# A gated recurrent mixer and a Walsh-Hadamard FFN on one core: row parts transposed by the DMA queue instead of TensorE, silu in one activation, new instruction orders

## The chip, the cores and the metric

The program runs on one core of a Trainium2 chip. The metric is the device time of one execution in microseconds. The core has TensorE (PE in the profile; its weight loads are PEld), VectorE (DVE), ScalarE (ACT), GpSimd (POOL) and SyncE (SP), which here issues every DMA.

## The reference

Input x is 4 batches x 512 rows x 512 columns, float32. With LN the layer norm without gain:

```
h = LN(x)
i, f, g = h Wi^T, h Wf^T, h Wg^T                 # 512 -> 512 each
gate = sigmoid(f);  v = silu(i) * (1 - gate)
o[t] = gate[t] * o[t-1] + v[t]                   # scan over the 512 rows of a batch
o = o * rsqrt(mean(o^2) + eps) * gnorm * g * sigmoid(g)
x = x + LN(o Wo^T)
z = LN(x)
hidden = fwht(silu(z W1^T) * (z W3^T))           # 512 -> 2048, Walsh-Hadamard over 2048
x = x + LN(hidden W2^T)                          # 2048 -> 512
```

## The kernel before, in words

**Numbers.** A float32 operand of a product is split into two float16 parts, high and low (low = value - high), and a product is three float16 passes into one PSUM bank: high x high, high x low, low x high (three_passes, L576 to L579). The transform fwht is folded into W2 once, in eight units (FW on GpSimd, H2 on TensorE, ScalarE and VectorE).

**Order.** Each engine runs a list of steps that stands written out at the top (PE_ORDER, ACT_ORDER, DVE_ORDER, POOL_ORDER, SP_ORDER, L37 to L186). A step is KIND.batch.index; in PE_ORDER a number behind a colon is its PSUM bank. Every step waits on semaphores for what it needs, and what stands behind it in its list waits with it. SP's list too is run in order, its waits included.

**Steps of a batch on TensorE.** XT transposes four 128-row tiles of normalised rows against the identity, in float32, four 128x128 blocks a tile. F, I and G (4 each) are the projections, 12 matmuls of 512 columns; MS sums squares; Y (4) is the product with Wo. ZT transposes the rows of the second norm. In batch 0, GA and UP (16 each, 12 matmuls) are the products with W1 and W3. In batches 1 to 3 each pair of column chunks is computed by seven products of half size, Strassen-Winograd's way: GP (6 matmuls of 256 columns), GQ, GR and GU (12 each), for 16 steps g, and ZT has seven steps: three of the rows' quarters and four of sums that GpSimd makes (ZA). D (64 a batch, three matmuls of 512 columns) is the product with W2.

**Around them.** Behind an XT or ZT step ScalarE copies the bank as the high part and VectorE subtracts for the low part, into xb or ring (L844, L932, L935; L1065, L1188, L1191). ScalarE computes sigmoid of F, I, G and GA (L869, L879, L901, L991); VectorE multiplies I, G and GA by their sigmoid (L1128, L1145, L1302), scans (S, L1140), multiplies the gate in (P, L1152). UP: VectorE multiplies, ScalarE rounds, GpSimd takes the low part (L1417). Row norms: VectorE's bn_stats (X1, Y, Z1, V), a GpSimd power (L1345), then VectorE or ScalarE applies them.

**Weights of the later batches.** SL loads the float32 weights of a chunk pair into comb_raw (L530), GpSimd forms four sums in place (SA, L1407 to L1413), ScalarE and VectorE split them (SH, SO), SS stores them to w_comb in DRAM; AS stores the plain parts. WL loads 1792 KB a pair into one of three slots of ring (L548).

**Other waits that matter.** The hidden parts of chunks 2 to 5 of batch 0 lie in xb[1], so batch 1's rows may be written there only after the sixth chunk's D (L842). GA.0.0 needs all of ZT.0, the weight scales (WS on VectorE) and WT.0.0. H2.0.0 needs neg_had (HN, L1288). GpSimd's unit 3 reuses the buffer of unit 0 and waits for H2.0.1 (L1386).

Of the kernel before, what the change touches and what calls it, by code (L numbers as in the profile page):

```python
# [42 lines left out]
GA.0.3:5 D.0.0 D.0.1 D.0.2 D.0.3 D.0.4 D.0.5 D.0.6 D.0.7 UP.0.3:6 D.0.8 D.0.9 D.0.10 D.0.11 GA.0.4:7 UP.0.4:5
D.0.12 D.0.13 D.0.14 D.0.15 GA.0.5:4 D.0.16 D.0.17 D.0.18 D.0.19 UP.0.5:6 GA.0.6:7 UP.0.6:5 GA.0.7:4 D.0.20
D.0.21 D.0.22 D.0.23 XT.1.0:6 XT.1.1:7 XT.1.2:5 XT.1.3:4 D.0.24 D.0.25 D.0.26 D.0.27 F.1.0:6 I.1.0:7 G.1.0:5
I.1.1:4 F.1.1:6 G.1.1:7 I.1.2:5 F.1.2:6 G.1.2:4 I.1.3:7 F.1.3:5 G.1.3:6 UP.0.7:4 GA.0.8:7 UP.0.8:5 D.0.28 D.0.29
D.0.30 D.0.31 MS.1.0:6 Y.1.0:4 Y.1.1:7 D.0.32 D.0.33 D.0.34 D.0.35 Y.1.2:5 Y.1.3:6 GA.0.9:4 UP.0.9:7 GA.0.10:5
UP.0.10:6 GA.0.11:4 D.0.36 D.0.37 D.0.38 D.0.39 ZT.1.0:7 ZT.1.1:5 ZT.1.2:6 UP.0.11:4 D.0.40 D.0.41 D.0.42 D.0.43
ZT.1.3:7 ZT.1.4:4 ZT.1.5:5 GA.0.12:6 D.0.44 D.0.45 D.0.46 D.0.47 ZT.1.6:7 UP.0.12:4 GA.0.13:5 UP.0.13:6 D.0.48
D.0.49 D.0.50 D.0.51 GA.0.14:7 UP.0.14:4 GA.0.15:5 UP.0.15:7 XT.2.0:6 XT.2.1:4 XT.2.2:5 D.0.52 XT.2.3:7 D.0.53  # L50
D.0.54 D.0.55 D.0.56 F.2.0:6 I.2.0:4 G.2.0:5 I.2.1:7 F.2.1:6 G.2.1:4 I.2.2:5 F.2.2:7 G.2.2:6 D.0.57 D.0.58
D.0.59 D.0.60 I.2.3:4 F.2.3:5 D.0.61 G.2.3:7 D.0.62 D.0.63 GP.1.0:6 GQ.1.0:4 GR.1.0:5 GP.1.1:6 GQ.1.1:7 GU.1.0:6
MS.2.0:4 Y.2.0:7 GR.1.1:5 GP.1.2:4 GQ.1.2:6 GP.1.3:4 GU.1.1:5 GQ.1.3:6 GR.1.2:7 Y.2.1:4 GR.1.3:5 GU.1.2:7
GP.1.4:6 D.1.0 GQ.1.4:5 GU.1.3:6 GP.1.5:7 Y.2.2:4 GQ.1.5:7 GR.1.4:6 GP.1.6:5 D.1.1 D.1.2 GQ.1.6:6 GR.1.5:5
GU.1.4:7 GP.1.7:4 D.1.3 Y.2.3:5 GQ.1.7:7 GR.1.6:4 D.1.4 GU.1.5:6 D.1.5 GP.1.8:5 GQ.1.8:4 GR.1.7:6 GU.1.6:5
GP.1.9:7 D.1.6 GQ.1.9:6 GR.1.8:7 GU.1.7:5 D.1.7 D.1.8 D.1.9 GR.1.9:5 D.1.10 D.1.11 D.1.12 D.1.13 D.1.14 D.1.15
D.1.16 D.1.17 D.1.18 GU.1.8:4 D.1.19 D.1.20 D.1.21 GP.1.10:7 GQ.1.10:6 GU.1.9:4 GP.1.11:5 GQ.1.11:7 GR.1.10:5
GP.1.12:4 GQ.1.12:6 GR.1.11:4 GU.1.10:5 GP.1.13:7 GQ.1.13:4 GR.1.12:5 GU.1.11:7 D.1.22 D.1.23 D.1.24 GP.1.14:7
D.1.25 D.1.26 D.1.27 D.1.28 D.1.29 D.1.30 D.1.31 D.1.32 D.1.33 D.1.34 GQ.1.14:6 GR.1.13:7 D.1.35 GU.1.12:5
# [24 lines left out]
D.3.55 D.3.59 D.3.63
# [103 lines left out]
def mixer_ffn_kernel(nc, x, w_i, w_f, w_g, w_o, gnorm, w_13t, w_2t, eye, hadamard, out):  # L188
# [15 lines left out]
    with ExitStack() as ctx:  # L204
# [370 lines left out]
        def _(pe):  # L575
# [885 lines left out]
```

## Time and profile before

| | us |
|---|---|
| median of 3 runs (731.03 to 731.64) | 731.22 |
| the profiled execution, whole | 729.96 |
| its span in the trace | 728.2 |
| PE busy / PEld busy | 700.3 (96%) / 427.9 |
| DVE busy | 519.2 (71%) |
| ACT busy | 285.4 (39%) |
| POOL busy | 311.1 (43%) |

Busy times are sums of instruction durations in the span. Matmuls overlap: one begins before the one ahead has ended, so a PE busy share near 100% says that it never ran dry, and the distance of starts says what a matmul costs. The chain of waits follows the last instruction back to what released it, step by step.

### The profile page before, as it was taken

What the parts mean: (1) busy time and instruction counts of PE and PEld (TensorE: products, weight loads), DVE (VectorE), ACT (ScalarE), POOL (GpSimd) and SP (SyncE); (2) the same over time, 40 slices, a digit from 0 to 9 for tenths busy, and PEclk for the clock granted to TensorE, in tenths of its full rate; (3) what the DMA queues carried; (4) which work ended last, traced back from release to release, by engine and by line L of the source; (5) the groups of instructions that cost most, each with busy time, mean ns of one, the idle gap of its engine ahead of it and who ended that gap; (6) DMA issues with size and microseconds to landing.
All of it is one profiled execution on the core that took longest, in us unless ns stands there. A gap on an engine that the chain in (4) does not pass through costs nothing.

```text
span 728.2 us, 11322 instructions
## 1 busy us (share of the span) xinstructions
PE 700.3 (96%) x4280; PEld 427.9 (59%) x4280; DVE 519.2 (71%) x877; ACT 285.4 (39%) x482; POOL 311.1 (43%) x268
## 2 busy tenths in 40 slices
PE   4898789999999999999999999999999999999996
PEld 2443334445444545467778677556666768876762
DVE  6997799895756765688755576885657765756564
ACT  5677844564443334343221332442312233313221
POOL 2967799453667843324341212241224530203112
PEclk9999979999999999999999999999999999999999
DMA  8961243364326475054252272432223332472002
GB/s 333 417 240 58 79 133 108 121 240 159 116 116 228 163 229 205 1 174 136 111 217 102 102 260 103 138 137 86 84 101 112 146 141 68 165 261 102 30 1 87
DMA packets 28199, 105.73 MB, mean 145 GB/s; under 512 B 2800, under 2 KB 7152, under 8 KB 23536
## 3 DMA queue, kind: packets, MB, share of 16 engines
q1 hardware_dynamic: 28144, 105.00, 40.7%
q8 instruction: 34, 0.56, 0.3%
q14 instruction: 21, 0.17, 0.1%
HBM read 81.92 MB, written 23.07 MB: 144 GB/s over the span
## 4 chain that ended last, share of the span: by engine, by line
PE 92%; DVE 4%; issue 1%; DMA 1%; ACT 0%; DVEq 0%; POOL 0%; SPq 0%
PE ps L577 28%; PE ps L578 28%; PE ps L579 28%; PE ps L751 2%; PE ps L752 2%; DVE ring L1086 1%; PE ps L719 1%; PE ps L629 1%; DVE st L1047 1%; DMA rows<-L_attn_hidden_states 1%; PE ps L686 0%; DMA x1r<-x_rows 0%; DVEq L1048 0%; DVE rows L1182 0%; DVE exps L1071 0%
## 5 line engine op out<-in xcount | busy, mean ns | idle before, releaser
L577 PE MATMUL ps<-xb,ring 128*128 128x256 f16 (+1 forms) x704 | 225.9, 321 | 0.1
L579 PE MATMUL ps<-xb,ring 128*128 128x256 f16 (+1 forms) x704 | 225.9, 321 | 0.0
L578 PE MATMUL ps<-xb,ring 128*128 128x256 f16 (+1 forms) x704 | 225.9, 321 | 0.0
L577 PEld LDWEIGHTS ps<-xb,ring 128*128 128x128 f16 x704 | 69.0, 98 | 45.9 <-issue 1.6
L578 PEld LDWEIGHTS ps<-xb,ring 128*128 128x128 f16 x704 | 68.9, 98 | 45.4 <-issue 1.0
L579 PEld LDWEIGHTS ps<-xb,ring 128*128 128x128 f16 x704 | 68.9, 98 | 42.1
L1345 POOL TENSOR_TENSOR rstd<-var,neg_half 128x1 f32<-128x1 f32 x64 | 43.8, 687 | 115.3 <-DVE var L1323 50.7
L1417 POOL TENSOR_TENSOR hsp<-sga,hsp 128x512 f16<-128x512 f32 x34 | 41.6, 1230 | 115.6 <-ACT hsp L1005 115.4
L579 PE MATMUL ps<-ring 128*128 128x256 f16 x288 | 78.5, 273 | 0.0
L577 PE MATMUL ps<-ring 128*128 128x256 f16 x288 | 78.5, 273 | 0.0
L578 PE MATMUL ps<-ring 128*128 128x256 f16 x288 | 78.5, 273 | 0.0
L1255 DVE TENSOR_TENSOR ring<-ps,ring 128x512 f32<-128x512 f32 x48 | 33.1, 689 | 29.7 <-PE ps L579 29.6
L991 ACT ACTIVATE sga<-ring,gate_c 128x512 f32<-128x512 f32 x48 | 34.5, 720 | 47.7 <-DVE ring L1266 36.1
L969 ACT ACTIVATE junk<-ps 128x256 f32<-128x256 f32 x48 | 18.4, 384 | 86.2 <-PE ps L579 86.2
L1302 DVE SCALAR_TENSOR_TENSOR sga<-ring,gate_c,sga 128x512 f32<-128x512 f32 x48 | 38.4, 803 | 19.0 <-ACT sga L991 19.0
L577 PE MATMUL ps<-w2t,hsp 128*128 128x512 f16 x136 | 51.5, 379 | 0.0
L578 PE MATMUL ps<-w2t,hsp 128*128 128x512 f16 x136 | 51.5, 379 | 0.0
L579 PE MATMUL ps<-w2t,hsp 128*128 128x512 f16 x136 | 51.5, 379 | 0.0
L1266 DVE TENSOR_TENSOR ring<-ps,ring 128x512 f32<-128x512 f32 x48 | 33.1, 689 | 25.8 <-PE ps L579 24.9
L1417 POOL TENSOR_TENSOR ring<-sga,ring 128x512 f16<-128x512 f32 x22 | 25.6, 1181 | 55.0 <-ACT ring L1005 55.0
L1245 DVE TENSOR_TENSOR ring<-ps,junk 128x512 f32<-128x512 f32 x48 | 32.9, 688 | 16.4 <-PE ps L579 13.7
L1314 DVE SCALAR_TENSOR_TENSOR sga<-ring,up_c,sga 128x512 f32<-128x512 f32 x48 | 41.2, 862 | 1.4 <-issue 0.2
(190 smaller groups left out, 1326.4 us busy)
## 6 DMA issues: line engine op xcount, KB each, us to landing
ring<-w_comb SPq DMA_DIRECT2D x24, 1792.0 KB, 7.3
ring<-W13t SPq DMA_DIRECT2D x16, 512.0 KB, 10.4
ring<-W13t SPq DMA_DIRECT2D x8, 1024.0 KB, 6.4
w_comb<-ring SPq DMA_DIRECT2D x8, 1024.0 KB, 8.5
rows<-L_attn_hidden_states SPq DMA_DIRECT2D x16, 256.0 KB, 4.0
w2t<-W2t SPq DMA_DIRECT2D x8, 512.0 KB, 13.6
res<-L_attn_hidden_states SPq DMA_DIRECT2D x16, 256.0 KB, 4.0
x_rows<-res SPq DMA_DIRECT2D x16, 256.0 KB, 3.0
```

The costliest lines, as they stand in the source:

```text
L577: pe.matmul(dst, a_hi, b_hi, start=start, stop=False)
L578: pe.matmul(dst, a_hi, b_lo, start=False, stop=False)
L579: return pe.matmul(dst, a_lo, b_hi, start=False, stop=stop)
L969: act.activation(p_copy[:, g % 2], bank("GP", b, g)[:, 256:512], ACT.Copy).then_inc(sp_rdy, 1)
L991: act.activation(sga[:, c % 2], src, ACT.Sigmoid, scale=gate_c[:]).then_inc(sga_rdy, 1)
L1245: dve.tensor_tensor(combined(g % 2)[:, 0:512].rearrange("p (o t) -> p o t", o=2), bank("GQ", b, g)[:].rearrange("p (o t) -> p o t", o=2), ...
L1255: dve.tensor_tensor(to[:, 512:1024].rearrange("p (o t) -> p o t", o=2), bank("GR", b, g)[:].rearrange("p (o t) -> p o t", o=2), both, ALU. ...
L1266: dve.tensor_tensor(to[:, 512:1024], bank("GU", b, g)[:], to[:, 512:1024], ALU.add).then_inc(gu_rdy, 1)
L1302: dve.scalar_tensor_tensor(sga[:, c % 2], src, gate_c[:], sga[:, c % 2], ALU.mult, ALU.mult).then_inc(sil_rdy, 1)
L1314: dve.scalar_tensor_tensor(sga[:, c % 2], src, up_c[:], sga[:, c % 2], ALU.mult, ALU.mult).then_inc(hid_rdy, 1)
L1345: pool.tensor_tensor(dst, src, neg_half[:].broadcast_to(src.shape), ALU.pow).then_inc(done, 1)
L1417: pool.tensor_tensor(hid(b, c, 1), sga[:, c % 2], hid(b, c, 0), ALU.subtract).then_inc(hid_lo, 1)
```

## The change

Batch 0 keeps its transposes on TensorE. In batches 1 to 3:

- XT and ZT on ScalarE and VectorE now split rows that are not transposed yet, in SBUF, into scratch of the attention part (si, sg, o_s, osq, osum, gate). SP then issues transposing DMAs, XD (4 a batch, 128 x 1024 float16 each) and ZD (7 a batch, each two of 128 x 512), into xb and ring. TensorE's 12 XT and 21 ZT steps of these batches are gone; F waits for XD, GP for ZD, and ScalarE's XT of batches 2 and 3 for all ZD of the batch before.
- GA, I and G use Silu, and VectorE's multiply by the sigmoid is gone; their bank is free after ScalarE. P multiplies the gain in as well. F's gate is 0.5 * tanh(f / 2) + 0.5 in two ScalarE steps.
- comb_raw has two places, ring slots 32 and 56 in turn. The three slots of WL are permuted.
- A few one-column VectorE steps change from three operands to two.
- All five orders are new.

```diff
+            def transpose_x(b, t):
+                sp.wait_ge(xt_lo, TC * b + t + 1)
+                if b == 1 and t == 0:
+                    sp.wait_ge(d_mm, EARLY)
+                if b > 1 and t == 0:
+                    sp.wait_ge(up_mm, HC * (b - 1))
+                sp.dma_start_transpose(xb[:, b % 2].rearrange("p s k t -> p (s k) t")[:, :, chunk(t)],
+                                       parts_of_x(t).rearrange("p s d -> p (s d)")).then_inc(ld_xt, 16)
+            def transpose_z(b, q):
+                sp.wait_ge(z_lo, z_count(b, q))
...
+                for i in range(2):
+                    sp.dma_start_transpose(place_of_z(b, q, i), parts_of_z(q)[:, i].rearrange("p s d -> p (s d)")
+                                           ).then_inc(ld_zt, 16)
 # TensorE
             def f(b, c):
+                if c == 0 and b > 0:
+                    pe.wait_ge(ld_xt, 16 * TC * b)
             def products_p1(b, g):
-                    pe.wait_ge(z_hi, z_count(b, 6))
-                    pe.wait_ge(z_lo, z_count(b, 6))
+                    pe.wait_ge(ld_zt, 32 * 7 * b)
 # ScalarE
             def xt(b, t):
+                if b > 0:
+                    act.wait_ge(x_norm, TC * b + t + 1)
+                    if b > 1:
+                        act.wait_ge(ld_zt, 32 * 7 * (b - 1))
+                    act.activation(parts_of_x(t)[:, 0], rows[:, t], ACT.Copy).then_inc(xt_hi, 1)
+                    return
             def f(b, c):
-                act.activation(gate[:, c % 2], bank("F", b, c)[:], ACT.Sigmoid, scale=unscale[:, 0:1]
+                act.activation(gate[:, c % 2], bank("F", b, c)[:], ACT.Tanh, scale=unscale[:, 0:1]
+                               ).then_inc(tanh_rdy, 1)
+                act.wait_ge(tanh_rdy, n + 1)
+                act.activation(gate[:, c % 2], gate[:, c % 2], ACT.Identity, bias=half[:], scale=0.5
                                ).then_inc(gate_rdy, 1)
-                act.activation(sga[:, c % 2], src, ACT.Sigmoid, scale=gate_c[:]
+                act.activation(sga[:, c % 2], src, ACT.Silu, scale=gate_c[:]
 # VectorE
             def xt(b, t):
+                if b > 0:
+                    dve.tensor_tensor(parts_of_x(t)[:, 1], rows[:, t], parts_of_x(t)[:, 0], ALU.subtract
+                                      ).then_inc(xt_lo, 1)
+                    return
-            def ga(b, c):
-                n = HC * b + c
-                dve.wait_ge(sga_rdy, n + 1)
-                src = combined(0)[:, c % 2 * 512:c % 2 * 512 + 512] if b > 0 else bank("GA", b, c)[:]
-                dve.scalar_tensor_tensor(sga[:, c % 2], src, gate_c[:], sga[:, c % 2],
-                                         ALU.mult, ALU.mult).then_inc(sil_rdy, 1)
 # weight sums, SP
                 if j == 0:
                     sp.wait_ge(up_mm, 2)
                     sp.wait_ge(st_a[0], 32)
+                elif j == 1:
+                    sp.wait_ge(up_mm, 8)
+                    for i in range(2):
+                        sp.wait_ge(st_a[i], 64)
                 else:
-                    sp.wait_ge(s_lo, 2 * j)
+                    sp.wait_ge(s_lo, 2 * j - 2)
```

From the new orders, the places that the prediction names:

```
PE_ORDER   XT.0.0:4 AN.0.0:5 XT.0.1:6 ... F.0.0:5 W2N.3.0 I.0.0:4 GC.0.0:6 F.0.1:1 ...
           G.0.1:5 AN.3.0:6 H2.0.0:4 H2.0.1:1 H2.1.0:7 I.0.2:2 F.0.2:3 F.0.3:6 G.0.2:0 I.0.3:5 H2.1.1:2
           G.0.3:4 H2.2.0:3 H2.2.1:6 H2.3.0:0 MS.0.0:5 Y.0.0:4 Y.0.1:1 Y.0.2:7 Y.0.3:2 ZT.0.0:5 H2.3.1:3
           H2.4.0:4 WS.0.0:1 H2.4.1:6 ZT.0.1:7 ZT.0.2:2 ZT.0.3:5 H2.5.0:1 H2.5.1:7 GA.0.0:2 UP.0.0:5 ...
           D.0.23 GA.0.8:4 D.0.24 ... D.0.28 UP.0.8:5 GA.0.9:6 F.1.0:7 I.1.0:4 ... MS.1.0:5 Y.1.0:6 Y.1.1:4
           Y.1.2:5 Y.1.3:7 D.0.36 D.0.37 UP.0.11:6 D.0.38 ... D.0.43 GA.0.12:4 UP.0.12:5 GA.0.13:6 D.0.44 ...
           GA.0.14:4 D.0.52 UP.0.14:5 GA.0.15:6 UP.0.15:7 D.0.53 ... D.0.61 GP.1.0:4 GQ.1.0:5 ... F.2.0:4
ACT_ORDER  AQ.0.0 XT.0.0 AQ.1.0 AT.0.0 XT.0.1 AQ.2.0 XT.0.2 XT.0.3 ... UP.0.15 XT.2.0 XT.2.1 XT.2.2 GP.1.0
DVE_ORDER  ... AT.0.2 HN.0.0 W2S.0.0 ... Z2.0.2 ZT.0.0 Z2.0.3 WS.0.0 ZT.0.1 ZT.0.2 ZT.0.3 WT.0.0 ...
POOL_ORDER ... P.0.0 FW.3.0 FW.3.1 FW.3.2 FW.3.3 FW.3.4 S.0.1 P.0.1 FW.3.5 ... Z1.0.3 FW.5.3 FW.5.4 FW.5.5 ...
SP_ORDER   ... SL.1.0 SL.2.0 AS.5.0 XD.1.0 XD.1.1 XD.1.2 XD.1.3 SL.3.0 ... ZD.1.0 ... ZD.1.5 XL.2.0 XL.2.1
           ZD.1.6 XL.2.2 XL.2.3 WL.1.0 WL.1.1 WL.1.2 XD.2.0 XD.2.1 XD.2.2 XD.2.3 WL.1.3 ...
```

## Rows read from the trace of the kernel before

**Rows 1.** The chain that ended last, by engine: share of the span.

```profile
PE 92%; DVE 4%; issue 1%; DMA 1%; ACT 0%; DVEq 0%; POOL 0%; SPq 0%
```

**Rows 2.** Stretches: length, busy time and instructions by engine, granted clock, DMA share, GB/s.

```profile
core 0: us, PE busy (x) PEld busy (x) DVE busy (x) ACT busy (x) POOL busy (x), PEclk, DMA share, GB/s
20.00:60.00 40.00, 35.07 (x190) 17.12 (x189) 38.95 (x58) 28.23 (x58) 29.82 (x20) 0.99 0.79 306
80.00:100.00 20.00, 13.31 (x44) 6.89 (x42) 18.29 (x51) 11.11 (x23) 17.16 (x18) 0.75 0.52 159
100.00:720.00 620.00, 620.00 (x3920) 388.09 (x3920) 432.29 (x701) 216.32 (x348) 239.55 (x206) 1.00 0.38 132
```

**Rows 3.** Timeline of PE, D steps near the end: start, duration, line, tile.

```profile
717.14 0.38 PE L579 MATMUL ps<-w2t,xb 128*128 128x512 f16 x1
...
719.08 0.38 PE L579 MATMUL ps<-w2t,xb 128*128 128x512 f16 x1
```

**Rows 4.** The chain in order of time: start, time on the chain, what.

```profile
594.48 0.44 PE ps L719 x4
...
639.98 0.11 PE ps L577
```

**Rows 5.** Groups by line and shape: busy us, mean ns, idle before; TensorE's transposes.

```profile
L629 PE MATMUL ps<-ident,rows 128*128 128x128 f32 x80 | 13.8, 319 | 15.2 <-DVE rows L1060 8.5 <-DVE rows L1182 6.7
L719 PE MATMUL ps<-ident,res 128*128 128x128 f32 x48 | 6.5, 273 | 0.0
L719 PE MATMUL ps<-ident,rows 128*128 128x128 f32 x36 | 5.1, 272 | 0.0
```

**Rows 6.** Groups by line and shape: the other engines' steps.

```profile
L1302 DVE SCALAR_TENSOR_TENSOR sga<-ring,gate_c,sga 128x512 f32<-128x512 f32 x48 | 38.4, 803 | 19.0 <-ACT sga L991 19.0
L1152 DVE TENSOR_TENSOR sg<-sg,o_s 128x512 f32<-128x512 f32 x16 | 16.2, 1014 | 0.2
L1128 DVE SCALAR_TENSOR_TENSOR si<-ps,unscale,si 128x512 f32<-128x512 f32 x16 | 11.9, 747 | 14.9 <-ACT si L879 14.9
L1407 POOL TENSOR_TENSOR ring<-ring 128x512 f32<-128x512 f32 x8 | 10.9, 1357 | 6.5 <-DMA ring<-W13t 6.5
L913 ACT ACTIVATE ot<-sg 128x512 f16<-128x512 f32 x16 | 10.0, 622 | 2.9 <-DVE sg L1152 2.7
```

**Rows 7.** DMA issues: count, KB each, median us from issue to landing.

```profile
ring<-w_comb SPq DMA_DIRECT2D x24, 1792.0 KB, 7.3
ring<-W13t SPq DMA_DIRECT2D x16, 512.0 KB, 10.4
rows<-L_attn_hidden_states SPq DMA_DIRECT2D x16, 256.0 KB, 4.0
ring<-L_attn_Wf SPq DMA_DIRECT2D x1, 1024.0 KB, 6.6
```

**Rows 8.** Line L514 (SP's weight loads): issue duration ns min/median/max, first and last start.

```profile
L514 SPq DMA_DIRECT2D ring<-W13t x16: 327/433/2936, 17.8 to 55.3; - x16
```

**Rows 9.** Timeline of PE before and at GA.0.0, with idle time before and its releaser.

```profile
58.71 1.55 PE L751 MATMUL ps<-x1r,had 128*128 128x512 f32 x2 [3.31 <-issue]
...
82.44 1.02 PE L751 MATMUL ps<-x1r,had 128*128 128x512 f32 x2
83.30 1.02 PE L752 MATMUL ps<-x1r,had 128*128 128x512 f32 x2
...
95.03 1.09 PE L629 MATMUL ps<-ident,rows 128*128 128x128 f32 x4 [0.83 <-DVE rows L1182]
...
101.71 0.38 PE L577 MATMUL ps<-xb,ring 128*128 128x512 f16 x1
```

**Rows 10.** Timeline of DVE: neg_had, and the first weight's low part.

```profile
58.40 0.22 DVE L1288 TENSOR_SCALAR neg_had<-had 128x128 f32<-128x128 f32 x1
...
100.49 1.08 DVE L1224 SCALAR_TENSOR_TENSOR ring<-ring,w_s 128x512 f16<-128x512 f32 x1
```

**Rows 11.** Timeline of POOL: the first step of unit 3.

```profile
64.23 2.51 POOL L1392 TENSOR_TENSOR x1r<-w2t 128x512 f32<-128x512 f32 x2 [2.16 <-PE ps L752]
```

**Rows 12.** Groups by line and shape: ScalarE's table loads.

```profile
L836 ACT ACT_TABLE_LOAD x1 | 1.3, 1283 | 0.7 <-PEq L1436 0.7
```

More of the change, by code:

```diff
@@ L43 @@
[L43 to L47, printed above, removed]
@@ L216, in mixer_ffn_kernel @@
         neg_half = sb("neg_half", [P, 1])
+        half = sb("half", [P, 1])
         warm = sb("warm", [P, 1])
@@ L343, in comb_z, with parts_of_x, parts_of_z, rows_of_z @@
             return flat[:, at:at + 512].rearrange("p (k t) -> p k t", k=2)
+        def parts_of_x(t):
+            return (si, sg, o_s, osq)[t][:].bitcast(F16).rearrange("p (s d) -> p s d", s=2)
+        def parts_of_z(q):
+            flat = (gate[:, 0], gate[:, 1], si[:], sg[:], o_s[:], osq[:], osum[:])[q]
+            return flat.bitcast(F16).rearrange("p (i s d) -> p i s d", i=2, s=2)
+        def rows_of_z(q):
+            if q > 2:
+                return comb_rows(q)
+            tiles, half = (0, 0, 2)[q], (0, 1, 1)[q]
+            return rows[:, tiles:tiles + 2, 256 * half:256 * half + 256]
+        def place_of_z(b, q, i):
+            if q < 4:
+                flat, at = xb[:, b % 2].rearrange("p s k t -> p (s k t)"), 1024 * q
+            else:
+                flat, at = ring, (98 if b % 2 else 40) * KB + 1024 * (q - 4)
+            return flat[:, at:at + 1024].rearrange("p (m t) -> p m t", m=4)[:, :, chunk(i)]
         def z_count(b, q):
@@ L704, in zt @@
                 wait_bank("ZT", b, t)
-                if b == 0:
-                    pe.wait_ge(z_norm, t + 1)
-                    transpose_tile(bank("ZT", b, t), rows[:, t]).then_inc(z_mm, 1)
-                    return
-                dst = bank("ZT", b, t)
-                if t < 3:
-                    pe.wait_ge(z_norm, TC * b + (4 if t == 2 else 2))
-                    tiles, half = (0, 0, 2)[t], (0, 1, 1)[t]
-                    src = rows[:, tiles:tiles + 2, 256 * half:256 * half + 256]
-                else:
-                    pe.wait_ge(z_cmb, TC * (b - 1) + t - 2)
-                    src = comb_rows(t)
-                for k in range(2):
-                    for i in range(2):
-                        last = pe.transpose(dst[:, 256 * k + P * i:256 * k + P * (i + 1)], src[:, i, chunk(k)], ident[:])
-                last.then_inc(z_mm, 1)
+                pe.wait_ge(z_norm, t + 1)
+                transpose_tile(bank("ZT", b, t), rows[:, t]).then_inc(z_mm, 1)
             def ws(b, t):
@@ L834, in _ @@
         def _(act):
-            act.wait_ge(half_set, 1)
-            act.activation(warm[:], neg_half[:], ACT.Sigmoid)
+            act.wait_ge(half_set, 2)
+            act.activation(warm[:], neg_half[:], ACT.Silu)
             def xt(b, t):
-                act.wait_ge(xt_mm, TC * b + t + 1)
-                if b == 1 and t == 0:
-                    act.wait_ge(d_mm, EARLY)
-                if b >= 2 and t == 0:
-                    act.wait_ge(up_mm, HC * (b - 1))
+                if b > 0:
[4 more added lines that the diff above has]
+                    return
+                act.wait_ge(xt_mm, t + 1)
                 act.activation(xb[:, b % 2, 0, :, chunk(t)], quarters(bank("XT", b, t)), ACT.Copy).then_inc(xt_hi, 1)
@@ L878, in i @@
                     act.wait_ge(o_rdy, n)
-                act.activation(si[:], bank("I", b, c)[:], ACT.Sigmoid, scale=unscale[:, 1:2]
+                act.activation(si[:], bank("I", b, c)[:], ACT.Silu, scale=unscale[:, 1:2]
                                ).then_inc(sgi_rdy, 1)
@@ L900, in g @@
                     act.wait_ge(o_lo, n)
-                act.activation(sg[:], bank("G", b, c)[:], ACT.Sigmoid, scale=unscale[:, 2:3]
+                act.activation(sg[:], bank("G", b, c)[:], ACT.Silu, scale=unscale[:, 2:3]
                                ).then_inc(sgg_rdy, 1)
```

417 lines of the change are left out of this document (209 added, 208 removed).

## The prediction, made before the changed kernel was run

> **What bounds the kernel now.** I read the shares of the chain first, then the stretches, then TensorE's own gaps. The chain that ended last is 92% TensorE [rows 1]. The stretches say where the rest lies: from 100 to 720 us TensorE is busy for all 620.00 us at the full clock, while VectorE is busy for 432 and ScalarE for 216 of them [rows 2]. In that part only less TensorE work makes the kernel shorter; a faster VectorE, ScalarE or GpSimd gives nothing there. Before 100 us it is different: PE is busy 13.31 of 20 us between 80 and 100, at a granted clock of 0.75, and VectorE 38.95 of 40 between 20 and 60 [rows 2].
>
> What TensorE's work costs is read from starts, not durations: a 512-column matmul lasts 0.38 us, but ten starts lie 1.94 apart, 0.2155 each [rows 3]; a 256-column one takes 0.11 of the chain [rows 4]. So F, I, G, Y, GA and UP are 12 x 0.2155 = 2.59 us each, D 0.65, GP 0.66, GQ, GR and GU 1.31 each; H2, two times 0.86 between starts [rows 9], 1.72. Four transposes take 0.44 us of the chain [rows 4]. Adding these along PE_ORDER, GA.0.0 stands at 72 us and the end at 692; in the trace GA.0.0 starts at 101.7 and the last work ends near 721.6. So 29.5 us are lost before GA.0.0 and next to nothing behind it.
>
> **Transposes off TensorE.** Removed: 3 batches x 4 XT steps x 4 = 48 and 3 x 7 ZT steps x 4 = 84 transposes, together 132; the 84 are the two forms of L719, and 48 of the 80 of L629 [rows 5]. 132 x 0.109 = 14.4 us. All of it stands where TensorE never idles, so all of it counts, if nothing is late in its place.
>
> The split moves ahead of the transpose: ScalarE copies rows instead of a bank (0.62 us, L913's form), and VectorE subtracts with both operands in SBUF; its nearest row is L1152, 1.01 us instead of 0.69 [rows 6]. 33 x 0.33 = +11 us of VectorE, against far more taken away below.
>
> **What the transposes cost the queue.** XD is 256 KB, ZD two transfers of 128 KB. The trace has no transposing transfer. Call c the queue's time for 256 KB. From below: 306 GB/s were moved on the mean of 20 to 60 us [rows 2], so 0.86 us; a queue that does nothing else may be somewhat quicker. From above: 512 KB of W13t take 10.4 us to landing, so 5.2 us for 256 KB [rows 7]. I take 1.3 us, nearer the lower end: a single 256 KB tile lands in 4.0 us [rows 7], most of it latency that four issued together share. What c may be is read from the work that stands between in the new orders:
> - XD.1 may start when D.0.23 is done (it writes where the early hidden chunks lie). Up to F.1.0 stand GA.0.8, UP.0.8, GA.0.9 and five D: 51 matmuls, 11.0 us, for 4c. At 1.3 plus a landing of 3 that is 8 us: hidden, and the tightest place.
> - Y.1.3 to GP.1.0: nine GA/UP and 26 D, 40.1 us. The norm chain takes some 14 us to the first split rows (in batch 0 the last ZT can start at 95.03 [rows 9], 12.6 us after the last Y's end at 82.44; GpSimd's row sums come behind that, while the first parts are already on their way). Then 7c, and behind them on the same queue WL.1.0, a w_comb load of 7.3 us [rows 7]. 14 + 7c + 7.3 = 30 us: hidden.
> - XD.2: UP.0.15 to F.2.0 is 37.6 us, with three w_comb loads ahead (22 us): leaves 15 for 4c. XD.3: GU.1.15 to F.3.0 26.7 us, two loads ahead: leaves 12. ZD.2 and ZD.3: 56 and 67 us.
>
> SP gets 54 more issues. By its plain issue, 0.43 us [rows 8], they are 23 us over 728; an upper end is the 2.9 us of its slowest one [rows 8], 157 us, still a fifth of the span. The new waits hold what is behind them: WL.1.0 waits behind ZD.1.6, and ScalarE's XT.2.0 waits for all ZD.1 with GP.1.0's copy behind it. GP.1.0 needs both anyway.
>
> The Trainium skill is at odds with itself here. "VectorE: DVE Perf Modes" (The three transpose paths) gives 390 ns for a 128x128 block on TensorE and 1309 ns through the DMA; eight blocks would make c 10.5 us. "Advanced Engine Details and Errata" (X-Bar Transpose) calls them as fast as regular DMAs. The trace prices TensorE's block at 109 ns, not 390, so I trust the first page's figures little as rates; no run here shows either yet.
>
> **One-activation gates.** GA loses its multiply (48 x 0.803 and 16 from a bank at L1128's 0.747, 50.5 us), I and G theirs (L1128's 11.9, and as much for G) [rows 6]: VectorE sheds 74 us and gains 11. F gets a second ScalarE pass, 16 x 0.62 = 10 us (L913's copy is the nearest) [rows 6]. Behind 100 us TensorE hides both signs: worth 0. If that cover were gone, the 0.62 would sit on the way to each scan.
>
> **Raw pairs.** The second buffer (over ring slots 56 to 63, free after UP.0.7) lets a load overlap four GpSimd sums of 1.36 or a little more each; GpSimd waited only 6.5 us in all for eight loads [rows 6]. Nothing of it is on the chain: worth 0, bounds -1 to +1 us. What it needs is that SS.7 is done before WL.1, 40 us earlier in TensorE's work than before (GP.1.0 moves from 286 to 247 in the sum). From UP.0.7 to there stand 121 us of work; seven pairs at about 6 us each take 42. Enough.
>
> **New orders, before GA.0.0.** Up to F.0.0 I expect nothing: Wf is issued behind four x tiles and lands 6.6 us later [rows 7], so squaring it first starts it little earlier, and XT.0.0 now stands behind it; bounds -1 to +1 us. Two gaps do change:
> - 3.31 us up to 58.71 [rows 9]. H2.0.0 waited for neg_had, written at 58.40 behind VectorE's gate work [rows 10]. In the new DVE_ORDER HN stands early and four H2 halves stand before G.0.3. The gap goes, and with it the slow clock behind it (two passes take 1.55 us there [rows 9]; about 1 us in all). What is late next is the gate chain: G.0.3 to ScalarE 0.7, VectorE 1.0, copy 0.6, GpSimd 1.4 and hand-overs, about 5; three H2 and MS (5.95 us) cover it. Gain 4.5 us.
> - From the last Y's end (82.44) to GA.0.0 at 101.71 [rows 9] are 19.3 us with 8.8 of work. VectorE's weight scales, two low parts and WT.0.0, done at 101.57 [rows 10], stand last. The new order leaves them there, so the time stays about 17.5, but 10.5 us of work stand in it (one more H2). GpSimd's unit 5 must be done by then: in the trace its unit 3 started only at 64.23, waiting for H2.0.1 [rows 11]; this now comes earlier. Idle falls from 10.5 to about 7: gain 3 us.
> Together 7 us, at the ends 2 (only the first gap, paid partly elsewhere) and 10.
>
> **Sum.** The profiled execution is 729.96 us, its span 728.2. 729.96 - 14.4 - 7 = 708.6, plus 1 us for a first wait at F.1.0 that the window of 11 us may just let through: 709.6. The median of the runs is 731.22, 1.26 above the profiled execution, so 710.9: **711 us**. Own range 704 to 718.
>
> **Rivals.**
> 1. *The queue's transposes are slow and TensorE waits for them.* For it: no row prices a transposing transfer, four in 11 us is tight, and loads queue behind them. Against: DMA is only 0.38 busy from 100 to 720 [rows 2]. Waits: F.1.0 4c - 11, GP.1.0 7c - 18.7, F.2.0 4c - 15, F.3.0 4c - 12. At the upper end, c = 5.2, that is 9.8 + 17.7 + 5.8 + 8.8 = 42: 711 + 42 = 753. It cancels the gain of 20 from c = 4.1 (5.4 + 10 + 1.4 + 4.4 = 21), so from about 4.2 us for 256 KB the kernel is slower. By the Trainium skill's 1309 ns a block (the page above) the same sum, with ZD.2 and ZD.3 late too, would give about 920; I give that 0.03 of the chance below. A mild form (c about 3.3) costs 8 to 10 us: 720.
> 2. *Silu and Tanh are not in one ScalarE table.* Then each F and the I behind it reload: 32 loads of 1.283 us [rows 12]. In batch 0 eight of them, 10.3 us, fall where ScalarE is busy 28.23 of 40 us [rows 2]; later ones are covered. About 8 us: 719. Against: in the trace one load serves Sigmoid, Square, Copy and Identity for the whole run [rows 12], so a table holds several functions. The Trainium skill's "ScalarE: Activation LUTs" (Table sets) names tanh beside sigmoid and does not place silu.
> 3. *The orders before GA.0.0 give nothing* (F.0.0 later since XT waits behind AQ.0.0, GpSimd's sixth unit late for H2.5): only the 14.4 stay: 717 to 718.
>
> **Chances.** Forecast 0.58, orders give nothing 0.12, mild queue wait 0.06, table 0.05, slow queue (above the old time) 0.19. Under 0.2% nothing can be told from no change (1.5 us); only a sliver between the mild and the slow queue lies there, 0.03, taken half from the slow case. So faster 0.79, same 0.03, slower 0.18. The range reaches from 703 into the slow case, to 738.
>
> **What would show it.** In the trace after: no L629/L719-like transposes after batch 0; TensorE busy in full from GA.0.0 to the end; its end near 700. GA.0.0 at about 95 to 98 us instead of 101.7 (its place in the new order is 3.4 us later, so the loss falls from 29.5 to 22). No gap before the first H2; Y.0.0 near 69. Landing of XD under 5 us and no TensorE wait on it at F.1.0; one table load. Wrong if TensorE idles at F.1.0 or GP.1.0 for the transposes, if more table loads appear, or if GA.0.0 is not earlier.

## The result, and the profile after

The changed kernel takes 721.78 us (median of 4 runs, 718.46 to 722.41) beside 731.12 us for the kernel before on the same chip: a ratio of 0.9867, 95% interval 0.9833 to 0.9901. It is faster by 9.3 us, where 20.2 were forecast. A second series on another chip gave 721.84 us, ratio 0.9888 (0.9872 to 0.9903). The profiled execution is one of 722.41 us, so the traces differ by 7.5 us.

The page of the changed kernel, busy time and share of the span by engine, then the chain that ended last by engine:

```profile
PE 689.6 (96%) x4148; PEld 414.3 (57%) x4148; DVE 469.3 (65%) x782; ACT 290.4 (40%) x498; POOL 322.2 (45%) x268
...
PE 77%; POOL 9%; DVE 5%; DMA 3%; issue 2%; SPq 2%; ACT 1%; POOLq 0%; DVEq 0%; ACTq 0%
```

TensorE held 92% of the chain [rows 1]; now it is 77%, and GpSimd has 9% where it had none. The same three stretches as in [rows 2]:

```profile
core 0: us, PE busy (x) PEld busy (x) DVE busy (x) ACT busy (x) POOL busy (x), PEclk, DMA share, GB/s
20.00:60.00 40.00, 34.27 (x171) 16.86 (x169) 36.46 (x53) 26.24 (x51) 33.02 (x22) 0.91 0.73 286
80.00:100.00 20.00, 16.21 (x60) 7.98 (x58) 16.88 (x49) 13.54 (x35) 17.96 (x19) 0.83 0.19 66
100.00:720.00 620.00, 610.44 (x3797) 374.17 (x3795) 390.28 (x634) 224.49 (x370) 246.51 (x206) 0.99 0.47 152
```

From 100 us on TensorE is no longer full. The stretch from 80 to 100 is fuller (16.21 us for 13.31), the one from 20 to 60 is not (34.27 for 35.07), and there the clock has fallen to 0.91.

To find each gap, the start of every step of PE_ORDER was laid against the price that the prediction gives it; what lies between two starts beyond that price is idle TensorE or slow clock. From the first instruction to the end of the last matmul:

| | before | after |
|---|---|---|
| GA.0.0 starts at | 101.7 | 105.2 (its place is 3.4 of work later) |
| lost before it | 29.5 | 29.6 |
| from GA.0.0 to the end | 620.0 | 609.3 |
| lost in that part | 0 | 7.3 |
| end | 721.7 | 714.5 |

Behind GA.0.0: 620.0 - 3.4 (H2.5, now ahead of it) - 14.4 + 7.3 = 609.5. The transposes' 14.4 us are there in full. The new orders won nothing before GA.0.0, and 7.3 us are newly lost behind it, in waits and in the slow clock after them: 6.0 from MS.1.0 to Y.1.2 at 226 to 236 us, 1.3 at D.0.56 at 281 us.

One trace tells the first part only roughly. The nine traces of kernels that have the changed kernel's early steps (it was profiled twice, and seven of the experiments below leave these steps alone) start GA.0.0 between 102.2 and 105.9 us, at 104.2 on the mean, and F.0.0 between 19.0 and 21.5. So the new early orders may be worth about 1 us, not 7.

The chain of waits of the changed kernel through the first of the new waits, in order of time (start, time on the chain, what):

```profile
175.73 1.16 ACT ring L1004
176.91 1.07 DVE ring L1266
178.11 1.29 DVE ring L1266
179.42 8.99 DMA ring<-W13t
188.47 2.13 POOL ring L1436
...
216.72 2.13 POOL ring L1440
218.93 1.60 POOL ring L1442
220.53 2.04 POOL ot L1392
222.56 1.11 POOL hsp L1446
223.68 1.69 POOL osum L1387
225.45 0.64 ACT osq L940
226.15 1.41 POOL osum L1387
227.70 1.02 PE ps L744 x8
228.73 1.03 issue
229.75 0.59 PE ps L633
230.34 0.43 PE ps L634
```

L1436 to L1442 are GpSimd's four passes of a weight sum (SA). The chain runs along them from 161.8 to 222: a sum, its split, the load of the next raw pair, the next sum. L1392 and L1387, the gate's low part (P) and the sum of squares (S) for which MS.1.0 and Y.1.0 wait, stand in the same queue behind SA.5 and SA.6. Two matmuls of TensorE in a row then start 0.43 us apart, twice the 0.2155 of [rows 3]: after the wait the clock is down. Stretches of the same trace around both large waits:

```profile
core 0: us, PE busy (x) PEld busy (x) DVE busy (x) ACT busy (x) POOL busy (x), PEclk, DMA share, GB/s
...
38.00:42.00 4.00, 0.00 (x0) 0.00 (x0) 3.93 (x5) 0.52 (x1) 3.92 (x3) 0.90 0.63 250
42.30:47.30 5.00, 5.00 (x14) 1.97 (x15) 3.16 (x7) 4.41 (x11) 2.83 (x3) 0.50 0.00 0
...
230.00:234.80 4.80, 4.80 (x12) 1.67 (x11) 0.00 (x0) 0.00 (x0) 4.56 (x4) 0.50 0.89 331
```

At a granted clock of 0.50, the 1.2 GHz level, a wait of 4.4 us at 38 to 42 costs 2.5 more behind it, and the two that make 3.0 before 230 (1.7 at MS.1.0, 1.3 at Y.1.0) cost 3.0.

### The profile page after: what moved, and what is told of

Read it like the earlier page. It is cut to its first block, busy times and chain, and to the rows that moved or that the text cites. A ratio compares the mean times of both kernels' runs of the same rounds, so it can differ in the third digit from the quotient of the medians.

```text
span 720.6 us, 11006 instructions
## 1 busy us (share of the span) xinstructions
PE 689.6 (96%) x4148; PEld 414.3 (57%) x4148; DVE 469.3 (65%) x782; ACT 290.4 (40%) x498; POOL 322.2 (45%) x268
## 4 chain that ended last, share of the span: by engine, by line
PE 77%; POOL 9%; DVE 5%; DMA 3%; issue 2%; SPq 2%; ACT 1%; POOLq 0%; DVEq 0%; ACTq 0%
PE ps L633 24%; PE ps L634 24%; PE ps L635 24%; PE ps L795 1%; PE ps L796 1%; DVE ring L1135 1%; SPq L563 1%; POOL ring L1440 1%; POOL ring L1438 1%; POOL ring L1436 1%; DMA ring<-W13t 1%; POOL ring L1442 1%; DMA ring<-L_attn_Wf 1%; POOL rstd L1374 1%; POOL ot L1392 1%
## 5 line engine op out<-in xcount | busy, mean ns | idle before, releaser
L1374 POOL TENSOR_TENSOR rstd<-var,neg_half 128x1 f32<-128x1 f32 x64 | 40.3, 638 | 103.8 <-DVE var L1100 38.6
L1446 POOL TENSOR_TENSOR hsp<-sga,hsp 128x512 f16<-128x512 f32 x34 | 42.0, 1238 | 98.5 <-ACT hsp L1049 98.5
L1446 POOL TENSOR_TENSOR ring<-sga,ring 128x512 f16<-128x512 f32 x22 | 26.1, 1193 | 100.4 <-ACT ring L1049 100.4
L1092 DVE BATCH_NORM_STATS2 st<-ps 128x6 f32<-128x512 f32 x32 | 22.2, 695 | 30.0 <-PE ps L635 30.0
L1392 POOL TENSOR_TENSOR ot<-sg,ot 128x512 f16<-128x512 f32 x16 | 24.2, 1515 | 34.2 <-ACT ot L961 34.1
```

Of the source, the lines that this page charges most:

```text
L1092: dve.bn_stats(st[:, which], src)
L1374: pool.tensor_tensor(dst, src, neg_half[:].broadcast_to(src.shape), ALU.pow).then_inc(done, 1)
L1392: pool.tensor_tensor(ot[:, 1, c, :], sg[:], ot[:, 0, c, :], ALU.subtract).then_inc(o_lo, 1)
L1446: pool.tensor_tensor(hid(b, c, 1), sga[:, c % 2], hid(b, c, 0), ALU.subtract).then_inc(hid_lo, 1)
```

## The experiments

Ratios are to the kernel before on the same chip; in us against its median there (729.6 to 730.2).

**Three transposes of four left out of the kernel before.**

```diff
-                for k in range(KC):
+                for k in range(first, KC):      # first = KC - 1 in batches 1 to 3; the ZT steps alike
```

> The kernel before, with one TensorE transpose instead of four in each of the 33 transposing steps of batches 1 to 3 (the splits read the one transposed quarter four times; three quarters of the transposed values are left out). Theory: TensorE has no idle time from GA.0.0 on, so each transpose is worth its 0.109 us and 99 of them 10.8 us: 720.3 us against 731.1. Rival (the slots of the transposes are covered by waits for the split, so the change got its 9.3 us elsewhere): within 2 us of 731.1.

Measured: 721.53 us, 0.9885 (0.9872 to 0.9898), 8.1 less. In its trace a step that was 0.44 us apart from the next is 0.11 in 26 of 33 cases, and the end comes 8.9 us earlier. So 0.109 is the price. The 1.9 us that came back stand right behind the other seven steps; for 0.8 of them the trace names what was waited for, a hidden part or a split, as here ahead of D.0.24 (timeline of PE: start, duration, line, idle before and its releaser):

```profile
166.16 0.60 PE L632 MATMUL ps<-ident,rows 128*128 128x128 f32 x4
167.27 0.38 PE L580 MATMUL ps<-w2t,hsp 128*128 128x512 f16 x1 [0.50 <-POOL hsp L1420]
```

**The gates alone, in the kernel before.** Sigmoid becomes Silu (I, G, GA) or Tanh and Identity (F), and DVE_ORDER loses its I, G and GA; Tanh's argument isn't halved.

> The kernel before, with the gates alone changed: Tanh and Identity for F, Silu for I, G and GA on ScalarE, VectorE's products I, G and GA left out (GS folded as in the changed kernel). Theory (VectorE is off the path that sets the end once TensorE is saturated; before GA.0.0 it is not): after GA.0.0 nothing; before it, VectorE's chain is 8 products x 0.7 to 1.7 us shorter and Y and Z start earlier: 727 to 731 us (before 730 to 731). Rival (gates are where the gain comes from): 722 to 725.

Measured: 729.19 us, 0.9987 (0.9978 to 0.9995): 0.4 to 1.6 us less, all of it before GA.0.0 (100.5 us for 101.7, though F.0.0 came 2.9 us later in that trace; why is open). VectorE's 74 us are worth nothing behind it.

**The old orders before GA.0.0, in the changed kernel.** The first splice put H2.5.0 directly ahead of GA.0.0, the second behind UP.0.0:

```diff
-... ZT.0.3:5 H2.5.0:1 H2.5.1:7 GA.0.0:2 UP.0.0:5 GA.0.1:0 ...
+... ZT.0.3:0 H2.4.0:1 H2.4.1:3 GA.0.0:7 UP.0.0:4 H2.5.0:2 H2.5.1:6 GA.0.1:0 ...
```

> The changed kernel, with the orders of the kernel before up to GA.0.0 on TensorE, ScalarE and VectorE and up to FW.4.5 on GpSimd (VectorE's gate products left out, as in the changed kernel). Theory (the new orders before GA.0.0 are worth nothing): idle TensorE before GA.0.0 as in the changed kernel, 29 to 30 us, GA.0.0 at 101 to 102 with H2.5.0 and H2.5.1 behind it: 721 to 722 us. Rival (the new early orders do give the 7 us that the prediction took): 727 to 729.

> The changed kernel with the orders of the kernel before up to GA.0.1 on TensorE and ScalarE, up to WT.2.0 on VectorE (gate products and X1.1.x left out) and up to FW.4.5 on GpSimd. In the first such run H2.5.0 stood directly ahead of GA.0.0 and waited 4.9 us there, which neither kernel has; here it stands behind UP.0.0, as in the kernel before. Theory (new early orders worth nothing): idle TensorE before GA.0.1 as in the changed kernel, 30 us: 721 to 722 us. Rival (worth some us): 724 to 728.

Measured: 724.85 us (0.9930), with 4.9 us of waits at H2.5.0 and H2.5.1 that neither kernel has; and 722.22 us, 0.9891 (0.9878 to 0.9904), beside 0.9888 of the changed kernel. GA.0.0 starts at 101.1 us and H2.5's 3.4 come behind it: 104.5 against 105.2. The new early orders are worth nothing, shown from that side.

**The early order mended.** On VectorE, W2D.0.0 waited behind a split (AT.1.2) and a scan (S.0.0):

```diff
-... GS.0.0 AT.1.2 S.0.0 W2D.0.0 AT.0.2 HN.0.0 ...
+... GS.0.0 W2D.0.0 AT.1.2 S.0.0 AT.0.2 HN.0.0 ...      # first run; and X2.0.0 before X1.0.3
+... AT.2.0 HN.0.0 ... GS.0.0 W2D.0.0 AT.1.2 S.0.0 ...  # second; X1/X2 as they were; PE: H2.3.1 before ZT.0.0
```

> The changed kernel, with two steps of VectorE's written order moved: X2.0.0 before X1.0.3 (as in the kernel before), and W2D.0.0 before AT.1.2 and S.0.0. Theory: the new early order pays back what it wins, at XT.0.0 (10.2 us against 8.2) and at W2S.0.0 (4.4 us of idle TensorE, then about 2.5 us at half clock). XT.0.0 is back at 8.2, the wait at W2S.0.0 goes; part of it comes back as a wait at H2.0.0 or the Z phase: 717.8 us, 4 less than the changed kernel (2 to 9 less). Rival (the stretch before GA.0.0 is bound by the chain of VectorE, ScalarE and GpSimd, whatever TensorE does): within 1 us of 721.8, GA.0.0 at 105.

> The changed kernel, with W2D.0.0 before AT.1.2 and HN.0.0 behind AT.2.0 on VectorE, and H2.3.1 before ZT.0.0 on TensorE. The run with W2D.0.0 moved and X2.0.0 back showed the wait at W2S.0.0 gone, a new one of 3.8 us at H2.0.0 for HN.0.0, and the wait at XT.0.0 only handed to AN.0.0. Theory: without HN's wait GA.0.0 starts at 97 (105.2 in the changed kernel, 102.1 in that run): 714 us. Rival (the chain of scans and splits on VectorE sets MS.0.0, and TensorE waits there instead): GA.0.0 at 101 to 103, 718 to 720.

Measured: 719.78 us, 0.9858 (0.9838 to 0.9878), and 720.51 us, 0.9874 (0.9860 to 0.9888). In the first trace the 4.4 + 2.5 us at W2S.0.0 are gone and H2.0.0 waits 3.8 + 1.6 for neg_had; GA.0.0 at 102.1. In the second neither waits, TensorE is busy for 39.62 of 40 us from 20 to 60, and MS.0.0 waits 3.6, then 3.4 at half clock; GA.0.0 at 104.5. The three traces with the first edit (that of the first run and two of the kernels that join the moves, below) start GA.0.0 at 101.4 to 102.6 us, 2.2 earlier on the mean than the nine without it. The second run's time is that of its rival. The wait moves along VectorE's chain: MS.0.0 waits for the fourth scan (66.06 to 68.13 us) and its square and sum, and VectorE is busy 38.91 of the 40 us:

```profile
20.00:60.00 40.00, 39.62 (x209) 19.69 (x207) 38.91 (x53) 28.02 (x54) 36.77 (x24) 1.00 0.71 276
```

**The last weight sums behind the Y phase of batch 1.**

```diff
-... UP.0.8 P.1.0 SA.5.0 P.1.1 S.1.1 SA.6.0 P.1.2 UP.0.9 S.1.2 S.1.3 S.2.0 P.1.3 SA.7.0 Y.1.0 ...
+... UP.0.8 P.1.0 P.1.1 S.1.1 P.1.2 UP.0.9 S.1.2 S.1.3 S.2.0 P.1.3 SA.5.0 Y.1.0 ... ZA.1.6 SA.6.0 UP.0.12 SA.7.0 UP.0.13
+... the same to ZA.1.6, then UP.0.12 SA.6.0 UP.0.13 SA.7.0           # second run
+... and UP.0.14 before X1.2.1, UP.0.15 before X1.2.3                 # third run
```

> The changed kernel, with the weight sums SA.5, SA.6 and SA.7 (and their SH, SO, SL, SS steps) behind P.1.3 and the Y phase of batch 1 in every engine's order, otherwise the same. Theory: MS.1.0 and Y.1.x wait for GpSimd's P.1.x and S.1.x, queued behind the sums; with them gone the 6 us between MS.1.0 and Y.1.2 go (1.7, 1.3, and 2.5 + 0.5 at half clock): 715.8 us. Rival (the sums then end too late: GQ.1.0 waits for the last store, at 284 us): 721 to 726, with a gap at GQ.1.0. Second rival (P.1.x is bound by ScalarE and VectorE, not by GpSimd's queue): 721.8, MS.1.0 still at 227.

> The changed kernel, with the weight sums SA.5 behind P.1.3, SA.6 behind UP.0.12 and SA.7 behind UP.0.13 on GpSimd, and their SH and SO steps behind the ZT and UP steps of their engines, so that neither the P, S, Y steps of batch 1 nor UP.0.12 stand behind a sum. Theory: in the first try with late sums the 6 us at MS.1.0 and Y.1.x did go, and came back as 13 us at D.0.48 and D.0.52, since SH.6.0 stood ahead of UP.0.12 and ZT.1.4 on ScalarE; without that only the first effect is left: 716 us, 5 to 6 less than the changed kernel. Rival (the sums and the transposing DMAs need all of the time up to GP.1.0, so every order has a wait of some 6 us somewhere before it): 720 to 724, with a gap between D.0.48 and GQ.1.0.

> As the run with the last weight sums set apart, and besides: on GpSimd UP.0.14 before X1.2.1 and UP.0.15 before X1.2.3, on ScalarE SH.7.0 behind UP.0.14, on VectorE SO.7.0 behind X1.2.3. In that run the stall at MS.1.0 and Y.1.x was gone and D.0.56 waited 4.2 us, and 2.4 us at half clock, for UP.0.14 on GpSimd, which stood behind the x statistics of batch 2. Theory (both waits are matters of the written order, and the work fits before GP.1.0): 714.5 to 716 us. Rival (the next one is GQ.1.0 or GP.1.2, for the last stored sum and the load behind it, since the chain of sums has no more room): 719 to 722.

Measured: 727.16 us (0.9961), 720.80 us (0.9880, 0.9862 to 0.9898), 719.59 us (0.9853, 0.9838 to 0.9868). In all three the 6 us from MS.1.0 to Y.1.2 are gone. The first lost 14.6 us from D.0.48 to GA.0.15, since ScalarE's SH.6.0 stood ahead of ZT.1.4 and UP.0.12. The second lost 6.6 at D.0.56. Its GpSimd (timeline: start, duration, line, idle before) did the x statistics of batch 2, L1371, ahead of UP.0.14, the L1443 at 273.94:

```profile
272.38 0.55 POOL L1371 TENSOR_TENSOR rstd<-var,neg_half 128x1 f32<-128x1 f32 x1 [4.32 <-DVE var L1097]
273.42 0.55 POOL L1371 TENSOR_TENSOR rstd<-var,neg_half 128x1 f32<-128x1 f32 x1 [0.50 <-DVE var L1097]
273.94 1.15 POOL L1443 TENSOR_TENSOR hsp<-sga,hsp 128x512 f16<-128x512 f32 x1
```

The third still waits 0.6 us at D.0.52 and 2.4 at D.0.60, and the 1.7 lost from D.0.61 to GR.1.0 are slow clock behind that wait:

```profile
280.40:283.50 3.10, 3.10 (x15) 2.00 (x14) 2.45 (x9) 0.38 (x1) 0.00 (x0) 0.50 1.03 431
```

So more than half of the 6 us came back before GP.1.0 was through, and the time is that of the rival; its cause is not seen there. VectorE waited 2.5 us for the store of the last sums, TensorE not at all.

**GpSimd's sums cut to 8 of 128 columns.**

> The changed kernel, with GpSimd's four passes of each weight sum on 8 of 128 columns per quarter (the sums are left out, all instructions and waits stay). Theory (GpSimd's 52 us of sums hold MS.1.0, and run beside VectorE they slow both engines: its pass took 1.26 us alone and 2.13 beside VectorE's, VectorE's split 1.24 to 2.2): the 7.3 us of idle TensorE after GA.0.0 go down to the 1.3 of D.0.56 or less, SO's pass on VectorE falls from 2.2 towards 1.3: 715.5 us. Rival (MS.1.0 waits for the scans of VectorE and ScalarE, not GpSimd): 720 to 722.

Measured: 716.15 us, 0.9804 (0.9791 to 0.9818), some 6 us below the changed kernel's 0.9888. The waits from MS.1.0 to Y.1.2 are gone and 3.0 us are left at D.0.56 and GP.1.0. Between the two profiled executions lie 4.5 us. The split behind the sums gets shorter on VectorE though it is untouched, by lines and shapes the changed kernel's and then this one's:

```profile
L1266 DVE SCALAR_TENSOR_TENSOR ring<-ring,w_s 128x1024 f16<-128x1024 f32 x16 | 30.6, 1950 | 2.3 <-ACT ring L1004 2.3
```

```profile
L1266 DVE SCALAR_TENSOR_TENSOR ring<-ring,w_s 128x1024 f16<-128x1024 f32 x16 | 23.4, 1505 | 6.1 <-ACT ring L1004 6.1
```

**One raw pair at a time.** One wait changed, and the same wait added for the second pair, which give a load the pace of a single buffer; SL.2.0 stands behind XD.1.3:

```diff
-                    sp.wait_ge(s_lo, 2 * j - 2)
+                    sp.wait_ge(s_lo, 2 * j)
```

> The changed kernel, where each load of a raw pair waits until the pair before it is summed and split (as with a single buffer), SL.2.0 put behind XD.1.3. Theory (the prediction's: the second pair is worth nothing in itself): within 1 us of the changed kernel. Rival (the sums' chain ends at the Y phase of batch 1, so each load of 4.5 to 9 us that is no longer hidden makes it later): 4 to 15 us slower, with the gap at GQ.1.0 or MS.1.0.

Measured: 754.13 us, 1.0331 (1.0317 to 1.0345): 32 us slower than the changed kernel beside it, twice the upper end of what the rival expected. The chain alternates between load and sum (start, time on the chain, what):

```profile
188.99 6.42 DMA ring<-W13t
195.48 1.27 POOL ring L1437
196.82 1.27 POOL ring L1439
198.16 1.27 POOL ring L1441
199.51 1.27 POOL ring L1443
200.81 1.16 ACT ring L1005
201.99 2.49 DVE ring L1267 x2
204.49 6.29 DMA ring<-W13t
```

15.5 us a pair; ScalarE waits for each sum with G and F queued behind. In these orders the second pair is necessary. With orders written for one pair it might cost less; that wasn't tried.

**The transposing DMAs in halves.**

```diff
-                sp.dma_start_transpose(xb[:, b % 2].rearrange("p s k t -> p (s k) t")[:, :, chunk(t)],
-                                       parts_of_x(t).rearrange("p s d -> p (s d)")).then_inc(ld_xt, 16)
+                for s in range(2):      # the ZD steps alike
+                    sp.dma_start_transpose(xb[:, b % 2, s, :, chunk(t)], parts_of_x(t)[:, s]).then_inc(ld_xt, 16)
```

> The changed kernel with each transposing DMA cut in two (the high and the low parts apart): the same bytes and blocks, 108 transfers instead of 54. Theory (about 1.3 us of the queue for each transfer, whatever its size): in batch 1 the ZD steps take 28 x 1.27 = 36 us of the queue instead of 18, and what stands behind them, the x loads with UP.0.14 and GP.1.0, is 18 us late, of which 1 to 3 us were waited already: 736 to 742 us, with the waits at D.0.56 or GP.1.0; F.1.0 5 us late besides, since four XD have 11 us and now take 10.6 and a landing. Rival (time by bytes): 720 to 723.

Measured: 760.00 us, 1.0408 (1.0385 to 1.0431). D.0.56 waits 19.7 us, F.1.0 2.1, and 15.3 more, which the theory did not give, stand in batch 2 from D.1.40 to D.1.46. The queue of SP (start, time, line, count), the changed kernel's XD and the halves' ZD of batch 1:

```profile
169.31 1.34 SPq L548 DMA_TRANSPOSE xb<-si  x1
171.09 1.23 SPq L548 DMA_TRANSPOSE xb<-sg  x1
```

```profile
256.25 11.58 SPq L564 DMA_TRANSPOSE xb<-gate  x8
267.88 5.11 SPq L564 DMA_TRANSPOSE xb<-si  x4
```

256 KB take 1.24 us on the median, 128 KB 1.27 (and in the chain below), 64 KB 1.25: the queue is charged for the transfer, not for its bytes.

**What stands behind the transposes on the queue.** The chain of the changed kernel before D.0.56:

```profile
272.05 1.19 SPq L563
273.28 1.27 SPq L563
274.60 2.96 DMA rows<-L_attn_hidden_states
277.59 0.69 DVE st L1092
278.80 0.55 POOL rstd L1374
279.35 1.13 POOL hsp L1446
```

The last ZD issues (L563), then an x tile of batch 2, its statistics on VectorE and GpSimd, and only then UP.0.14 (L1446). The edit puts UP.0.14 and UP.0.15 ahead of these statistics and WL.1.0 ahead of the x loads.

> The changed kernel with UP.0.14 and UP.0.15 ahead of the x statistics X1.2.0 and X1.2.2 on VectorE (X1.2.1 on GpSimd), and the first load of combined weights (WL.1.0) ahead of the x loads of batch 2 on the queue. Theory: the queue spends 17.6 us on 14 transposes of batch 1, one after the other at 1.26 each; the x loads and WL.1.0 stand behind them, VectorE waits 9 us for the x tile with UP.0.14 behind it, and D.0.56 waits for that. Nothing of it is needed: the 1.3 us at D.0.56 goes, and none comes at GP.1.0: 1 to 2 us less than the changed kernel beside it. Rival (GP.1.0 waits for the last transpose itself): no change, the wait stands at GP.1.0.

Measured: 724.18 us, 0.9923 (0.9909 to 0.9937), slower than the changed kernel beside it by 2.3 us. Its profiled run is its fastest, 722.17; there D.0.56 no longer waits and D.0.60 waits 2.9. What the other runs lost is open.

**The moves together.**

> Both sets of moves together (VectorE's two early steps, the last three weight sums behind the Y phase of batch 1). Theory: the two stalls are apart in time and add: 711.8 us (range 707 to 716). Rival (idle time in front of a saturated TensorE moves along: what is gained early is waited for at the weight sums): about 716.

> Both of the two kernels above together. Theory: the stalls are 100 us apart and add: 708 us. Rival (an earlier TensorE only waits longer for the weight-sum chain of batch 1): 713 to 716.

> The changed kernel itself once more, beside the three others. Both theories: 718.5 to 722.5 us, ratio to the kernel before 0.984 to 0.990.

> All moves that the runs so far point to: W2D.0.0 before AT.1.2 and X2.0.0 before X1.0.3, the sums SA.5 to SA.7 apart from P, S, Y and UP of batch 1, UP.0.14, UP.0.15 and WL.1.0 ahead of the x tiles of batch 2. Theory: 3 us before GA.0.0 and 5 to 7 after it: 8 to 10 us less than the changed kernel beside it, 712 to 714. Rival (the stalls move along): no more than 3 us less.

Measured: 726.74 us (0.9954), 721.78 us (0.9890), the changed kernel again 721.84 us (0.9888), and the last 717.76 us, 0.9836 (0.9822 to 0.9849). The first carries the fault of its first late sums, the second that of D.0.56 (4.2 us, then 2.4 at half clock) and the wait at MS.0.0. The last beats both kernels: 4.1 us less than the changed kernel beside it, about half of the 8 to 10 expected and a little more than its rival's 3. Its GA.0.0 starts at 101.4 us (103.8 in the kernel beside it); D.0.60 waits 3.6 and GR.1.1 1.9, the second for VectorE's GQ.1.0, which comes behind VectorE's other steps and, by 0.2 us, the store of the last sums. Behind the wait at D.0.60 the granted clock stays full:

```profile
278.00:281.00 3.00, 3.00 (x30) 2.68 (x29) 3.00 (x6) 1.86 (x4) 1.14 (x1) 1.00 0.54 218
```

## Why the prediction was right or wrong

- *Transposes off TensorE, -14.4 us.* Right, in the size too: 620.0 - 3.4 - 609.3 + 7.3 = 14.6 us, and 0.109 each in the run that left 99 out. The sentence "if nothing is late in its place" carried the rest.
- *New orders, before GA.0.0, -7 us.* Wrong: 0 (29.6 us lost for 29.5; 722.22 us with the old ones). The first gap went as forecast, H2.0.0 starts at 47.9 us without a wait. The step that failed is "What is late next is the gate chain". The next was W2S.0.0, 4.4 us with 2.5 at half clock behind it, for VectorE's W2D.0.0 behind a split and a scan: VectorE was full from 20 to 60 us [rows 2], the prediction itself says so, and each step moved up on it pushes another back. F.0.1 waited 1.3 more, and F.0.0 came 1.1 later. Y.0.0 came at 76.4 us, not near 69. The second gap was nearly right: the three waits of ZT.0.1 to ZT.0.3 (7.7 us) became one of 4.0 at ZT.0.0 and small ones, and of the 10.5 idle us from the last Y's end to GA.0.0 7.9 were left, a gain of 2.6 for the 3 forecast. (The whole stretch took 18.5 us; that it "stays about 17.5" doesn't follow from the 19.3 before.) Rival 3 named this outcome and its time, 717 to 718, for a kernel without the next item. Of its reasons F.0.0 was later; H2.5 waited 0.7 us, for VectorE and not for GpSimd's sixth unit.
- *Raw pairs, "worth 0, bounds -1 to +1 us", "42 of 121 us. Enough".* Wrong, and the second step that failed: +6.0 us. The sum compared the sums' length with their deadline at WL.1.0. What counts is what stands behind them on an in-order engine: P.1.x and S.1.x, for which TensorE waits some 55 us before that deadline. Nor was a pair 6 us: a pass took 1.54 to 1.71 on the mean, up to 2.24, so 6.6 us, and up to 9 more where the load was not hidden. And the second pair, costed at nothing, is worth 32 us in these orders.
- *The queue, c = 1.3 us for 256 KB, +1 us at F.1.0.* c is 1.3 for most XD and 2.5 for ZD, since the charge is 1.3 for each transfer. Two of the twelve XD, the first of batch 2 behind three w_comb loads, held the queue 5.3 and 5.8 us. F.1.0, F.2.0 and F.3.0 do not wait. Rival 1 fell: c was above its 4.2 for these two alone, and nothing waited for them. At GP.1.0 "14 + 7c + 7.3 = 30" left the x loads out, which queue behind 18 us of ZD with UP.0.14 behind their statistics; that is 1.3 us in one trace of the changed kernel and 2.5 in the other. By the Trainium skill's page "VectorE: DVE Perf Modes" (The three transpose paths) a 128x128 block through the DMA takes 1309 ns. As a price of each block the traces don't bear it out: eight blocks (XD) took 1.24 us of the queue on the median and landed in 3.3, four blocks (ZD) 1.27 and 2.5, and the 920 us never came. As the queue's price of a whole transfer it is close.
- *Gates, 0.* Right behind 100 us; before it 0.4 to 1.6 us, which the prediction left out. Rival 2 fell: one table load stands in the trace after, of 1.28 us.

So 709.6 for the profiled execution, less the 1 us at F.1.0 that didn't come, plus 7 for the orders and 7.3 for the waits in batch 1: 722.9, and it was 722.41. The time lies in the range of 703 to 738, but the gain is less than half of the forecast.

## What to carry to other kernels

When work leaves a saturated engine, all of its time comes back only if no other in-order engine was using that time. So for each batch work of a helper (here the weight sums), ask what stands behind it in its queue and when the saturated engine wants that, not when the batch itself must be done. Where the clock fell behind a wait, the wait cost up to twice its length (4.4 + 2.5, 3.0 + 3.0, 2.4 + 1.7 us); behind one of 3.6 it did not fall. A step moved up on a full engine can move another back by as much.

## What the runs showed of the hardware that was not expected

- VectorE and GpSimd slow each other down when VectorE reads both inputs from SBUF. GpSimd's pass of a sum took 1.26 us alone and 2.13 beside VectorE's split, and VectorE's split 1.27 and 2.29; passes of VectorE that read a bank and SBUF stayed at 0.69 on the mean of 48, beside GpSimd too. The split rows of this change read SBUF twice where they read a bank before: 0.99 us on the mean of 33 (the prediction took 1.01), between 0.68 and 1.78, and 1.25 for 0.69 in the worst group:

```profile
L1224 DVE TENSOR_TENSOR gate<-rows,gate 128x512 f16<-128x512 f32 x6 | 7.3, 1246 | 0.0
```

  The Trainium skill's "SBUF — State Buffer" (Who interferes with whom) says that a VectorE instruction with two SBUF inputs contends with a GpSimd instruction that reads SBUF. The traces agree. neg_had, a tensor_scalar with one input, took 1.28 us for the 0.22 of [rows 10]: it began at 42.99 us while a GpSimd step ran and ended at 44.27, the step at 44.19. The same section names tensor_scalar among the operations that can enter a two-port mode and then contend; whether this one did, no trace shows.
- A transposing DMA holds SP's queue for 1.17 to 1.34 us in 47 of 54 cases here and 99 of 108 in halves, at 64, 128 and 256 KB alike; most plain issues take 0.33 to 0.5. Right behind three loads of 1792 KB two took 5.3 and 5.8 us. Merging a ZD's two transfers into one might halve its charge; it wasn't tried.
